# Ternary feed-forward layer: clamps of the quantised activations left out, the rounding constant taken off by ScalarE

## The reference, cut to what matters

```python
def bitlinear(x, W, b):
    w_scale = jnp.clip(jnp.mean(jnp.abs(W)), EPS, None)
    Wq = _ste(W, jnp.clip(jnp.round(W / w_scale), -1.0, 1.0) * w_scale)
    x_scale = jnp.clip(jnp.max(jnp.abs(x), axis=-1, keepdims=True), EPS, None)
    xq = _ste(x, jnp.clip(jnp.round(x * (QB / x_scale)), -QB - 1.0, QB) * (x_scale / QB))
    return jnp.einsum('bnd,hd->bnh', xq, Wq) + b
h = bitlinear(x, W1, b1)              # 256 -> 1024
h = jax.nn.gelu(h, approximate=False)
return bitlinear(h, W2, b2)           # 1024 -> 256
```

## Time and profile before

| | |
|---|---|
| time, median of 3 runs | 4466.64 us (4465.85 to 4473.64) |
| the profiled execution's own time | 4502.6 us |
| its span, first to last instruction | 4500.8 us |
| busy: PE, DVE, ACT, POOL | 78%, 51%, 33%, 9% of the span |
| granted TensorE clock, mean | 0.869 of full speed |
| L1 stages, first L2065 to the last L2101 | 58.45 us in each of the four batches |

### The profile page before, as it was taken

How to read it: one execution, slowest core, us unless ns; L and a number is a source line. 1 busy time by engine, 2 the same in 40 slices (tenths; PEclk the granted TensorE clock), 3 DMA queues, 4 the chain that set the end, 5 groups by cost and what they waited for, 6 DMA issues and landing times.

```text
span 4500.8 us, 51861 instructions
## 1 busy us (share of the span) xinstructions
PE 3497.8 (78%) x20322; PEld 1826.0 (41%) x20322; DVE 2298.6 (51%) x4977; ACT 1488.1 (33%) x2106; POOL 390.4 (9%) x298
## 2 busy tenths in 40 slices
PE   5278677667767749999778888788787896878969
PEld 2133332332332336666434433345343452444524
DVE  8765465565465335555463443643436534355343
ACT  2124333433334323333243322443224432234322
POOL 6000001001000124444200000000000000000000
PEclk7668868967877869999889989999899998999989
DMA  3221221231131056555401222012211113011130
GB/s 121 85 56 16 100 57 16 69 88 16 36 121 16 19 121 140 141 141 141 88 10 25 30 54 48 11 25 28 57 32 26 25 25 60 25 34 25 25 60 10
DMA packets 203902, 249.63 MB, mean 55 GB/s; under 512 B 99985, under 2 KB 166179, under 8 KB 191781
## 3 DMA queue, kind: packets, MB, share of 16 engines
q1 hardware_dynamic: 183945, 222.06, 19.3%
q0 software_dynamic: 19712, 24.20, 3.4%
HBM read 167.53 MB, written 77.25 MB: 54 GB/s over the span
## 4 chain that ended last, share of the span: by engine, by line
PE 53%; DVE 25%; ACT 7%; DMA 7%; issue 5%; SPq 2%; POOL 1%; another core or an unknown queue 1%; DVEq 0%; ACTq 0%; POOLq 0%
PE ps L806 5%; PE ps L808 5%; PE ps L807 5%; PE ps L1342 5%; DVE max_parts L1992 4%; PE ps L859 4%; PE ps L991 3%; PE ps L953 3%; PE ps L1199 2%; PE ps L1206 2%; PE ps L974 2%; ACT arena L1512 2%; PE ps L1127 2%; DVE minus_max_context L2136 2%; DMA q_stack<-scr_q 1%
## 5 line engine op out<-in xcount | busy, mean ns | idle before, releaser
L859 PE MATMUL ps<-ternary_W,ident 128*128 128x512 f16 x1552 | 496.2, 410 | 80.5 <-issue 25.4
L1992 DVE TENSOR_REDUCE max_parts<-ps 128x1 f32<-128x512 f32 (+3 forms) x768 | 388.5, 551 | 251.4 <-PE ps L956 151.8
L1444 ACT ACTIVATE arena<-ps 128x256 f32<-128x256 f32 (+7 forms) x512 | 321.4, 650 | 508.3 <-PE ps L974 289.2
L953 PE MATMUL ps<-k_stack,q_stack 96*128 96x512 f16 (+3 forms) x768 | 272.5, 390 | 101.0 <-DVE max_parts L1992 57.6
L1912 DVE CAST arena<-arena 128x512 f16<-128x512 f32 (+2 forms) x296 | 143.0, 483 | 316.1 <-ACT arena L1607 201.0
L974 PE MATMUL ps<-q_stack,k_stack 98*128 98x512 f16 (+3 forms) x768 | 257.6, 382 | 39.8 <-ACT arena L1444 24.4
L1512 ACT ACTIVATE arena<-ps 77x1024 f32<-77x1024 f32 x192 | 190.4, 1016 | 279.3 <-PE ps L1119 274.4
L859 PEld LDWEIGHTS ps<-ternary_W,ident 128*128 128x128 f16 x1552 | 153.4, 104 | 314.8 <-issue 113.7
L2414 DVE TENSOR_REDUCE max_parts<-ps 128x1 f32<-128x512 f32 x256 | 170.1, 688 | 176.1 <-PE ps L1317 174.1
L1342 PE MATMUL ps<-arena 128*96 128x512 f32 x512 | 246.1, 592 | 1.7 <-ACT arena L1671 1.7
L1914 DVE TENSOR_TENSOR arena<-arena 128x512 f16<-128x512 f32 (+2 forms) x296 | 239.0, 808 | 10.2
(11 more groups left out here) (429 smaller groups left out, 7059.8 us busy)
## 6 DMA issues: line engine op xcount, KB each, us to landing
arena<-scr_expert_weights SPq DMA_DIRECT2D x46, 1024.0 KB
q_stack<-in_exp_W SPq DMA_DIRECT2D x16, 1024.0 KB
scr_expert_weights<-k_stack SPq DMA_DIRECT2D x16, 1024.0 KB, 4.9
q_stack<-scr_q SPq DMA_DIRECT2D x120, 128.0 KB, 3.8
scr_q<-arena SPq DMA_DIRECT2D x48, 256.0 KB, 2.9
k_stack<-scr_q SPq DMA_DIRECT2D x72, 128.0 KB, 4.1
scr_q<-arena SPq DMA_DIRECT2D x16, 512.0 KB, 4.3
scr_k<-arena SPq DMA_DIRECT2D x16, 512.0 KB, 4.5
```

Of the source, the lines that this page charges most:

```text
L859: pe.matmul(s[:, 0:CH], ident[:], Wq1[:, 0, 0:CH], start=True, stop=True)
L953: mm = pe.matmul(s[:, 0:n], QS[0:MROW, buf, j, t * P:(t + 1) * P], KS[0:MROW, buf, j, c * CH:c * CH + n], start=True, stop=not on_edge)
L1444: act.activation(PR[:, n % NP, kt * P:T], slot(L, "ST", g, kt, j)[:, kt * P:T], ACT.Exp).then_inc(*did("act", L, "exp", g, kt, j))
L1992: dve.tensor_reduce(mpart[:, j * NT + t, c:c + 1], slot(L, "S", g, t, j, c)[:, 0:n], AX, ALU.max).then_inc(*frees("dve", L, "S", g, t, j, c))
```

## The change

Three edits. In ternary_input DVE stops after xr1: both clamps of all four tiles go, eight instructions a chunk. In their place ACT, at its step XQ, adds -MAGIC to two tiles at a time (128x512) and writes xq, two instructions a chunk; PE's transposes then wait for ACT instead of DVE. In quantise the clamp hr2 goes, one instruction a tile, and ACT's HR waits for hr1.

```diff
@@ PE, step XQ
-                        pe.wait_ge(*of("dve", "L1", "xq", c, t))
+                        pe.wait_ge(*of("act", "L1", "xq", c, t // 2 * 2))
@@ ACT, step XQ
+                    for t in range(0, TCH, 2):
+                        act.wait_ge(*of("dve", "L1", "xr1", c, t + 1))
+                        act.activation(xq[c][:, t:t + 2], XNc[c][:, t:t + 2], ACT.Identity, bias=epsc[:, 2:3], scale=1.0).then_inc(*did("act", "L1", "xq", c, t))
                     act.wait_ge(*of("pe", "L1", "XQ", c))
@@ ACT, step HR
-                    act.wait_ge(*of("dve", "L1", "hr2", c, t))
+                    act.wait_ge(*of("dve", "L1", "hr1", c, t))
@@ DVE, ternary_input
                     dve.tensor_scalar(XNc[c][:, t], XNc[c][:, t], sm[:, n:n + 1], MAGIC, ALU.mult, ALU.add).then_inc(*step("L1", "xr1", c, t))
-                for t in range(TCH):
-                    dve.wait_ge(*of("dve", "L1", "xr1", c, t))
-                    dve.tensor_scalar(XNc[c][:, t], XNc[c][:, t], -MAGIC, QB, ALU.add, ALU.min).then_inc(*step("L1", "xr2", c, t))
-                for t in range(TCH):
-                    dve.wait_ge(*of("dve", "L1", "xr2", c, t))
-                    dve.tensor_scalar(xq[c][:, t], XNc[c][:, t], -QB - 1.0, None, ALU.max).then_inc(*step("L1", "xq", c, t))
@@ DVE, quantise
                 dve.tensor_scalar(hr[c][:, t % 2], hb[c][:, t % 2], sm[:, m_:m_ + 1], MAGIC, ALU.mult, ALU.add).then_inc(*step("L1", "hr1", c, t))
-                dve.wait_ge(*of("dve", "L1", "hr1", c, t))
-                dve.tensor_scalar(hr[c][:, t % 2], hr[c][:, t % 2], MAGIC - QB - 1.0, MAGIC + QB, ALU.max, ALU.min).then_inc(*step("L1", "hr2", c, t))
```

## The result

The kernel after took 4426.93 us (median of 6 runs, 4423.49 to 4434.74) against 4466.25 us before (6 runs, 4458.35 to 4474.84): a ratio of 0.9915, 95% interval 0.9898 to 0.9931, 38 us less with 7.5 us on either side. The forecast was 4429.0 us. The profiled execution took 4426.14 us, its span was 4424.4 us.

What follows compares the result with a forecast made beforehand. The prediction took DVE to bound the L1 stages. Gains of 2.2 (input), 5.8 (hr2) and 1.4 us (clock) made 9.4 us a batch, 37.6 us in all, so 4466.64 became 4429.0 us; range 4417 to 4446.

Steps and rivals of the forecast that it cites:

- The bound: In the middle of the first L1 stage DVE is the bound, busy 34.2 of 36 us, PE 25.3.
- Part 1: In ternary_input, DVE's removed clamps and ACT making xq bring the first H1 earlier: gain 2.2 us a batch.
- Part 2: In quantise, removing hr2 gains 0.73 us of DVE time for each of eight tiles, 5.8 us a batch.
- cover of 2.0 us: Slack left on the return path from hr2 over ACT and PE's H2 to DVE's L2197, so no new wait.
- rival B: No difference: PE's fillers or H2 become the bound and DVE's saving turns idle; 4458 to 4468 us, chance 0.07.
- Part 3: Around H1 in the L1 stage, fewer low spells of PE's clock: gain 0 to 2.2, taken as 1.4 us a batch.
- the second gap is 3.16 - 0.73 = 2.4 us, like the one after which the clock was high: PE's idle gap before a later H1 shrinks to 2.4 us; its low spell of 1.75 us for H1 mostly goes.
- The sum: For the L1 stages, 9.4 us a batch, 37.6 us in all, giving a median of 4429.0 us.
- DVE's idle time before h below 3 us a batch: Sign expected in the profile after: DVE waits less for H1 ahead of h, from 3.9 to below 3 us a batch.
- A: Only DVE's mid-stage time is won, the handover to ACT gives back the input's saving: 4443.5 us, chance 0.18.
- C: Slower: PE's granted clock falls outside the stage, at a mean of 0.89 the kernel needs 4478 us; chance 0.04.
- D: More than forecast: both low spells go and H2 at the stage's end runs high, 46 us, 4421 us, chance 0.11.

Runs made afterwards that it cites:

- after again: The kernel after, unchanged, run a second time beside the kernel before on the same chip: ratio 0.9893.
- input only: The kernel after with the clamp hr2 put back, so only the input's clamps are gone: ratio 0.9966 to the kernel before.
- before again: The kernel before, unchanged, run again as a control: median 4508.55 us, ratio 1.0013.
- 26 fillers: The kernel after with 26 fillers instead of 14 on PE ahead of chunk 0's XQ: ratio 0.9903 to the kernel before.

## Why the prediction was right, point by point

**The bound.** DVE bounds the stage: shown from both sides, 5.1 us for seven hr2 less and 5.1 us for seven more, besides idle time before h.

**Part 1, the clamps of the input.** Right to 0.1 us. L2173 starts right behind xr1, chunk 1's search for the largest magnitude starts 6.81 us after chunk 0's instead of 8.43, 1.62 less. ACT's instruction took 710 ns (0.72 forecast), PE waited 4.09 us ahead of chunk 0's XQ (4.0 forecast), and with the low state, as before, the first h comes 13.63 us after the stage's start instead of 15.84: 2.21 us (2.2 forecast).

**Part 2, hr2.** Right. hr1 to the next instruction is 0.67 us (2276.76 to 2277.43), 0.73 less than before, eight times a batch. No wait took its place: DVE has no idle time before QZ, and before the H2 sums (L2192) it has 3.8 us over the kernel against 4.3 before, all of it at the last sum of each batch. The cover of 2.0 us on the way back from PE was enough, the point on which rival B hung.

**Part 3, the granted clock.** Here a term was mis-sized, and one step of it was wrong. I took 1.4 us a batch: half of the first low spell and most of the second. The stage with 2.2 us and seven hr2 gone would be 50.35 us; measured were 49.66, 49.64, 49.71 and 47.95, so the clock gave about 0.7 us in three batches and 2.4 in the fourth, 1.1 on average, and the fourth is above the upper end of 2.2 us. The failing step is "the second gap is 3.16 - 0.73 = 2.4 us, like the one after which the clock was high". After idle 2.43 us H1 took 1.40 us where the first H1 had been low, and after 2.45 us 1.03 where it had been high. In the fourth batch of after again it took 1.03 us after idle 2.43 us although the first H1 had been low. The length of one gap doesn't decide it, and what does is not shown. What was forecast as a middle is a choice between two cases, 0.7 and 2.4 us, and which one comes changes from batch to batch and from execution to execution with the same program (one of four, then two of four).

**The sum.** 36.6 us from the stages of the first trace, against 37.6 forecast and 38 (31 to 46) measured. The agreement of the medians to 2 us is luck beyond what the terms deserve: the interval is 7.5 us on either side, and the share of high batches, which the forecast could not know, moves the sum by 1.7 us a batch. The sign "DVE's idle time before h below 3 us a batch" did not follow from the forecast's own terms, which give 3.5. The trace alone would have misled: its span fell by 76 us, 33 of them ahead of the third phase.

**The rivals.** A falls (input only gained 2.2 us a batch or more), B falls by the missing idle time. C is not seen: the stretches behind the stages are not longer, and their granted clock (the third value from the end) is the same or above. Behind the first stage, before and after, then behind the fourth, before and after:

```profile
2352.00:2868.40 516.40, 434.45 (x2293) 219.56 (x2291) 211.26 (x478) 162.46 (x199) 0.00 (x0) 0.92 0.17 35
2309.00:2825.00 516.00, 434.76 (x2301) 220.50 (x2300) 212.68 (x482) 164.22 (x200) 0.00 (x0) 0.92 0.17 35
...
4073.00:4500.80 427.80, 358.97 (x1811) 181.30 (x1811) 172.32 (x378) 131.87 (x162) 0.00 (x0) 0.93 0.16 31
4001.00:4424.40 423.40, 355.26 (x1812) 179.48 (x1811) 171.74 (x378) 131.97 (x162) 0.00 (x0) 0.94 0.16 32
```

From the last hr1 of each batch to the next stage or the end, the four stretches sum to 1979.0 us before and 1985.9 before again, 1968.6 after and 1969.7 after again. That is less by more than the four last hr2, but the other kernels without hr2 lie between 1968.9 and 1986.8, so no more than the last hr2's 0.73 us a batch is claimed. D holds for single batches only: in the fourth the first H1, the later one and the H2 at the stage's end all ran high. From its first L2068 to the last sum into x_tokens (L2192) it took 54.0 us, 11.3 less than the fourth batch before; D had 11.5.

## What to carry to other kernels

Find the stretch in which one engine bounds, and count what the change takes off that engine there, start to start: the page's shares did not move, and 33 us of the difference between two traces lay ahead of the change and did not come back in others. An instruction can be handed to an idle engine even when it comes later there, if the consumer behind it has cover; where the engine that hands over is the bound, the handover gained 2.2 us a batch, and the same operation kept on that engine about 1 us less. Where a matmul on the path may run at either clock, forecast two cases instead of their middle; filling both of PE's gaps ahead of it, not one, went with a high clock in all four batches of the one execution, which the whole time didn't show.

## What the runs showed of the hardware that was not expected

- The granted clock can differ between batches with the same instructions and the same gaps. After idle gaps of 4.09 and 0.65 us the first H1 was high in one batch of after again and low in another; in the first trace of after the low spell of the high batch had begun earlier and ended earlier. With 26 fillers, equal rows up to the idle 2.13 us were followed by high in two batches and low in two. So the clock fell with no idle gap of PE above 2.13 us in the stretch.
- A low first H1 costs 1.26 us at once (3.67 against 2.41 us from xr1 to h). In the two traces of after the batches with it also had 0.3 to 0.6 us more idle time of DVE before later h (0.50 to 0.75 against 0.16 us), mostly at a later slowed H1.
- An Identity of 128x512 from SBUF with a bias from a tile took 706 ns in the median (710 on average), a Copy of the same shape without one 618 ns. The Trainium skill (ScalarE: Activation LUTs, What ACT_TABLE_LOAD costs) gives 280 ns and 0.833 ns an element with such a bias, an estimate of 707 ns, and 186 ns and 0.833 ns an element with scale and bias as constants, an estimate of 613 ns; both agree. The prediction had taken 0.72 us, between its rows of 618 and 1148 ns.
